# Reordering the opening of a one-core AdaLN transformer layer: split row load, another queue for one weight, stack transfers shared 6 and 6, value products placed among the row maxima, and a new written order for the first batch

## The reference

```python
mod = (silu(c) @ wmod)                      # 8 x 6 x 256: sa, ca, ga, sb, cb, gb
h = layernorm(x) * (1 + ca) + sa
qkv = h @ w_qkv                             # 16 heads of width 16
scores = q @ k.T / 16, causal, softmax      # 16 heads x 1024 x 1024
x = x + ga * ((softmax @ v) @ w_o)
h = layernorm(x) * (1 + cb) + sb
shared = (silu(h @ w1.T) * (h @ w2.T)) @ w3.T          # hidden 1024
routed = top 2 of 8 experts of hidden 256, gated by a sigmoid
x = x + gb * (shared + routed)
```

## Time and profile before

| What | us |
|---|---|
| median of 3 runs | 1855.86 |
| profiled execution, its own time | 1855.64 |
| its span, first to last instruction | 1853.8 |
| TensorE busy / VectorE busy / ScalarE busy / GpSimd busy | 1718.1 / 1580.6 / 1074.0 / 913.8 |
| mean granted TensorE clock | 0.964 |

### The profile page before, as it was taken

How to read it: one execution, slowest core, us unless ns; L and a number is a source line. 1 busy time by engine, 2 the same in 40 slices (tenths; PEclk the granted TensorE clock), 3 DMA queues, 4 the chain that set the end, 5 groups by cost and what they waited for, 6 DMA issues and landing times.

```text
span 1853.8 us, 46094 instructions
## 1 busy us (share of the span) xinstructions
PE 1718.1 (93%) x17630; PEld 992.5 (54%) x17630; DVE 1580.6 (85%) x2889; ACT 1074.0 (58%) x1346; POOL 913.8 (49%) x1003
## 2 busy tenths in 40 slices
PE   5578889999999999999999999999999999899896
PEld 2223445545554455545454545455544888678674
DVE  7889999998998898999889988998896777556787
ACT  2568767666766676767666766776665333222321
POOL 2123356455545654545545555546455467444433
PEclk8598899999999999999999999999999999999998
DMA  4234321303121312122212121222213667767998
GB/s 148 54 131 133 109 58 49 90 17 89 42 64 42 90 44 67 40 88 42 65 30 87 42 65 39 79 42 82 53 43 119 165 135 158 155 161 157 267 321 289
DMA packets 214133, 183.14 MB, mean 99 GB/s; under 512 B 146640, under 2 KB 182232, under 8 KB 212128
## 3 DMA queue, kind: packets, MB, share of 16 engines
q1 hardware_dynamic: 200768, 143.87, 30.4%
q0 software_dynamic: 12960, 36.06, 5.8%
q10 hardware_dynamic: 192, 0.26, 0.1%
HBM read 65.23 MB, written 62.19 MB: 69 GB/s over the span
## 4 chain that ended last, share of the span: by engine, by line
PE 54%; DVE 19%; POOL 8%; issue 6%; SPq 5%; DMA 5%; ACT 4%; ACTq 0%; DVEq 0%; POOLq 0%
PE pair L1892 11%; PE pair L1884 11%; DVE max_part L1319 9%; PE pair L1936 6%; PE pair L1862 6%; PE pair L1916 5%; PE pair L1838 5%; PE pair L1812 3%; POOL lists L983 3%; PE pair L1927 2%; PE pair L1824 2%; ACT arena L1129 2%; POOL slots L998 2%; PE pair L1962 1%; POOL hidden L1004 1%
## 5 line engine op out<-in xcount | busy, mean ns | idle before, releaser
L1129 ACT ACTIVATE arena<-pair 128x1024 f32<-128x1024 f32 (+1 forms) x640 | 570.1, 938 | 206.7 <-PE pair L1862 200.8
L1319 DVE TENSOR_REDUCE max_part<-pair 128x2 f32<-128x1024 f32 (+2 forms) x448 | 532.8, 1214 | 38.8 <-PE pair L1838 36.7
L1892 PE MATMUL pair<-feat_parts,ffn_sb 128*128 128x512 f16 x1536 | 379.1, 381 | 8.4 <-DVE silu_h L1367 2.9
L1884 PE MATMUL pair<-arena,v_sb 128*32 128x256 f32 (+1 forms) x5120 | 324.0, 374 | 3.4 <-POOL arena L916 1.5
L916 POOL TENSOR_SCALAR_AFFINE_SELECT arena<-arena 128x512 f32<-128x512 f32 x256 | 161.7, 647 | 228.9 <-ACT arena L1129 228.4
L922 POOL TENSOR_SCALAR_AFFINE_SELECT arena<-arena 128x1024 f32<-128x1024 f32 x128 | 141.3, 1104 | 248.8 <-ACT arena L1111 248.6
L1838 PE MATMUL pair<-arena 48*128 48x128 f16 (+3 forms) x2304 | 207.5, 284 | 34.8 <-DVE max_part L1319 10.6
L1862 PE MATMUL pair<-arena 50*128 50x256 f16 (+1 forms) x2560 | 212.8, 266 | 27.0 <-ACT arena L1129 13.9
L1892 PEld LDWEIGHTS pair<-feat_parts,ffn_sb 128*128 128x128 f16 x1536 | 130.8, 98 | 175.8 <-issue 29.9
L1916 PE MATMUL pair<-parts,arena 128*128 128x256 f16 x1704 | 201.3, 277 | 14.0 <-DMA parts<-lists 11.1
L998 POOL DMA_INDIRECT slots<-arena,feat x142 | 144.4, 1017 | 137.8 <-DVE arena L1556 105.6
(11 more groups left out here) (218 smaller groups left out, 2160.9 us busy)
## 6 DMA issues: line engine op xcount, KB each, us to landing
arena<-parts SPq DMA_DIRECT2D x380, 64.0 KB, 2.3
rows<-x SPq DMA_DIRECT2D x8, 1024.0 KB, 5.6
x_sb<-x SPq DMA_DIRECT2D x16, 512.0 KB
base<-norm SPq DMA_DIRECT2D x14, 512.0 KB, 3.3
ffn_parts<-hidden SPq DMA_DIRECT2D x8, 768.0 KB, 4.1
arena<-ffn_parts SPq DMA_DIRECT2D x8, 768.0 KB, 6.6
x_sb<-ffn_w SPq DMA_DIRECT2D x6, 768.0 KB, 5.5
norm<-ffn_w SPq DMA_DIRECT2D x6, 768.0 KB, 7.0
```

The lines of the kernel that those rows point to most:

```text
L1129: sc.activation(to[:, :, lo:QC], of[:, :, lo:QC], ACT.Exp, scale=SCALE / QK_SCALE ** 2).then_inc(exp_done, 1)
L1319: return vec.tensor_reduce(to, of, AX.X, ALU.max)
L1884: last = mm(to[32 * j:32 * j + 32, lo:QC], v_sb[:, kt, h:h + 32], probs[:, u % RING, at + lo:at + QC], start=(kt == 0), stop=(kt == 2 * c ...
L1892: last = mm(to[:, 0:512], w_up[s][W_PART[i]][:, f, m * RH + h * P:m * RH + (h + 1) * P], feat_parts[:, A_PART[i], f, c * 512:(c + 1) * 512 ...
```

## The change

- The rows of batch 0 come in two transfers of 512 KB, each with a semaphore, and the statistics of each half wait only for their own.
- `wmod_sb` is sent from ScalarE's queue, ahead of its first instruction, instead of from SyncE's.
- Of the 8 row tiles VectorE normalises 0 to 3, and ScalarE 4 to 7.
- The first 12 stack transfers go 6 and 6 (`FIRST_BY`).
- In the start, `v:0` and `v:1` stand behind the eighth maximum (`V_BEHIND = 8`) instead of ahead of the first; `take_v` stands behind `shifts`; `split` of group 1 stands between the maxima 3 and 4. The banks of the start are others.
- The order and the banks of "first" are others. "second" and all that follows is unchanged.

```diff
-FIRST_SENT = 4
+FIRST_BY = ((0, 6), (6, 12))
 "first":
-        max:1:0 max:1:1 max:1:2 max:1:3 share:0 share:1 select_max:1:1 qk:2 scores:0 max:1:4 max:1:5 scores:1 diag_max:1:1 scores:2 scores:3 values:0 values:1
-        raw:0 max:1:6 max:1:7 max:1:8 select_max:1:5 scores:4 diag_max:1:5 scores:5 scores:6 select_max:1:10 select_max:1:14 max:1:9 max:1:10 max:1:11
-        max:1:12 max:1:13 diag_max:1:10 max:1:14 scores:7 values:2 max:1:15 max:1:16 max:1:17 share:2 share:3 diag_max:1:14 values:3 values:4 values:5
-        values:6 scores:8 normalise:0 scores:9 raw:1 load_x1 shifts:1 max:2:0 scores:10 scores:11 scores:12 scores:13 values:7 values:8 values:9 values:10
-        values:11 raw:2 normalise:1 normalise:2 max:2:1 max_turn:1 mods scores:14 max:2:2 scores:15 values:12 scores:16 gates_out scores:17 values:13 guards
+        load_x1 select_max:1:1 max:1:0 max:1:1 max:1:2 max:1:3 max:1:4 share:0 qk:2 scores:0 scores:1 max:1:5 diag_max:1:1 raw:0 normalise:0 values:0 values:1
+        share:1 select_max:1:5 select_max:1:10 scores:2 scores:3 max:1:6 max:1:7 max:1:8 diag_max:1:5 max:1:9 scores:4 scores:5 max:1:10 max:1:11 scores:6
+        max:1:12 values:2 select_max:1:14 max:1:13 diag_max:1:10 max:1:14 values:3 values:4 max:1:15 max:1:16 max:1:17 share:2 share:3 scores:7 values:5
+        values:6 scores:8 scores:9 scores:10 scores:11 scores:12 values:7 values:8 diag_max:1:14 shifts:1 max:2:0 max:2:1 raw:1 normalise:1 values:9 values:10
+        values:11 scores:13 max_turn:1 mods scores:14 scores:15 scores:16 scores:17 scores:18 values:12 values:13 raw:2 normalise:2 values:14 values:15
+        values:16 guards scores:19 scores:20 scores:21 max:2:2 raw:3 select_max:2:1 values:17 values:18 values:19 max:2:3 raw:4 scores:22 values:20 values:21
...
-    "start": "0246024602460246024602460"
+    "start": "0246024024024026262626262"
...
-WORK["start"] = [("turn", 0), ("turn", 1), ("qk", 0), ("qk", 1), ("v", 0), ("v", 1)]
-WORK["start"] += [("max", 0, p) for p in range(MAXES)] + [("max_turn", 0)]
+V_BEHIND = 8
+WORK["start"] = [("turn", 0), ("turn", 1), ("qk", 0), ("qk", 1)] + [("max", 0, p) for p in range(V_BEHIND)]
+WORK["start"] += [("v", 0), ("v", 1)] + [("max", 0, p) for p in range(V_BEHIND, MAXES)] + [("max_turn", 0)]
...
 # SyncE
-            load_x1(0)
-            sp.dma_start(wmod_sb, w_mod[:, :, 0:2 * D]).then_inc(mod_in, 16)
+            for h in range(2):
+                t = slice(4 * h, 4 * h + 4)
+                sp.dma_start(rows[:, t, :], x_v[0][:, t, :]).then_inc(x1_first[h], 16)
...
-            stack(0, 0, FIRST_SENT)
+            sp.wait_ge(part_low, at_group(0, 0))
+            for to, of in first_stack(0):
+                sp.dma_start(to, of).then_inc(stacked[0], 16)
             stack(0, 1)
 # ScalarE
+            sc.dma_start(wmod_sb, w_mod[:, :, 0:2 * D]).then_inc(mod_in, 16)
...
+            act.wait_ge(std1_ready, 1)
+            for t in range(NT // 2, NT):
+                sc.activation(rows[:, t, :], rows[:, t, :], ACT.Identity, bias=rstd[:, 2, t:t + 1], scale=rstd[:, 1, t:t + 1]).then_inc(norm1_act, 1)
...
 # VectorE
-            dve.wait_ge(x1_in, 16)
             for h in range(2):
+                dve.wait_ge(x1_first[h], 16)
                 spread(0, rows, 4 * h, 4 * h + 4, var1_ready)
...
-            for g in range(EARLY):
-                split(0, "start", g)
-            for h in range(2):
-                take_v(0, "start", h)
+            split(0, "start", 0)
             for p in range(MAXES):
+                if p == 4:
+                    split(0, "start", 1)
                 if not OF_DIAG[p]:
                     maxima(0, "start", 0, p)
...
             shifts(0, 0, 0)
+            for h in range(2):
+                take_v(0, "start", h)
```

More of the change, by code:

```diff
@@ L138 @@
[L138 to L149, removed]
@@ new lines @@
+        scores:23 spread1:0 max:2:4 scores:24 scores:25 select_max:2:5 scores:26 diag_max:2:1 max:2:5 max:2:6 max:2:7 values:22 gates_out max:2:8 diag_max:2:5
+        select_max:2:10 values:23 share:4 scores:27 scores:28 spread1:1 scores:29 scores:30 values:24 values:25 values:26 values:27 max:2:9 max:2:10 max:2:11
+        max:2:12 max:2:13 diag_max:2:10 select_max:2:14 share:5 values:28 qk:3 normalise:3 normalise:4 values:29 max:2:14 values:30 scores:31 scores:32
+        scores:33 values:31 raw:5 raw:6 max:2:15 max:2:16 scores:34 scores:35 max:2:17 norm1 scores:36 values:32 load_gates diag_max:2:14 normalise:5
@@ new lines @@
+        normalise:6 scores:37 values:33 scores:38 turn:0 scores:39 values:34 values:35 values:36 shifts:2 select_max:3:1 max:3:0 max_turn:2 max:3:1 max:3:2
+        max:3:3 max:3:4 select_max:3:5 max:3:5 raw:7 diag_max:3:1 values:37 values:38 values:39 share:6 scores:40 scores:41 scores:42 turn:1 max:3:6 raw:8
+        values:40 values:41 max:3:7 scores:43 scores:44 max:3:8 diag_max:3:5 select_max:3:10 max:3:9 scores:45 max:3:10 max:3:11 share:7 select_max:3:14 qk:0
+        normalise:7 raw:9 values:42 scores:46 scores:47 values:43 values:44 values:45 scores:48 scores:49 max:3:12 max:3:13 diag_max:3:10 max:3:14 max:3:15
@@ new lines @@
+        scores:50 values:46 values:47 values:48 values:49 share:8 scores:51 scores:52 scores:53 max:3:16 values:50 normalise:8 normalise:9 scores:54 scores:55
+        scores:56 select_max:0:1 max:3:17 diag_max:3:14 raw:10 values:51 values:52 scores:57 values:53 shifts:3 max:0:0 max:0:1 scores:58 max_turn:3
+        normalise:10 values:54 values:55 max:0:2 max:0:3 share:9 qk:1 scores:59 scores:60 values:56 values:57 values:58 max:0:4 scores:61 scores:62 values:59
+        scores:63 scores:64 raw:11 diag_max:0:1 max:0:5 max:0:6 max:0:7 max:0:8 values:60 values:61 select_max:0:5 select_max:0:10 raw:12 share:10
@@ new lines @@
+        diag_max:0:5 max:0:9 max:0:10 v:0 v:1 scores:65 max:0:11 scores:66 normalise:11 max:0:12 share:11 load_x:0 values:62 values:63 scores:67 values:64
+        scores:68 scores:69 values:65 max:0:13 max:0:14 values:66 values:67 scores:70 scores:71 select_max:0:14 diag_max:0:10 max:0:15 values:68 max:0:16
+        scores:72 max:0:17 values:69 scores:73 raw:13 scores:74 values:70 scores:75 normalise:12 raw:14 normalise:13 values:71 normalise:14 diag_max:0:14
+        shifts:0 values:72 values:73 scores:76 scores:77 scores:78 values:74 scores:79 values:75 max_turn:0
@@ L356 @@
     assert next(banks, None) is None, v
-DVE_SETUP = 23
+DVE_SETUP = 22
 DVE_FIRST = 43
@@ L536, in adaln_layer @@
         x1_in, x_in = sem("x1_in"), [sem(f"x_in{h}") for h in range(2)]
+        x1_first, std1_ready, norm1_act = [sem(f"x1_first{h}") for h in range(2)], sem("std1_ready"), sem("norm1_act")
         gates_in, part_done, x_scaled = sem("gates_in"), sem("part_done"), sem("x_scaled")
@@ L1232, in _ @@
             act.wait_ge(part_low, at_group(0, 0))
[L1233 to L1236, removed]
+            for to, of in first_stack(1):
+                sc.dma_start(to, of).then_inc(stacked[0], 16)
             part_hi(0, "start", 1)
@@ L1648, in batch @@
                         if at[0] == 0:
[L1649 removed]
+                            dve.wait_ge(x1_in, (b + 1) * 16)
                             dve.wait_ge(feat1_ready, at_half(b, 1))
@@ L1680, in _ @@
             vec.tensor_copy(mod_sb, misc[0:B, :]).then_inc(setup_read, 1)
-            norm1(0, 0)
+            dve.wait_ge(inv1_ready, 1)
+            vec.scalar_tensor_tensor(rstd[:, 2, :], mean_var[:, :, 0], -1.0, rstd[:, 1, :], ALU.mult, ALU.mult).then_inc(std1_ready, 1)
+            dve.wait_ge(std1_ready, 1)
+            for t in range(NT // 2):
+                vec.tensor_scalar(rows[:, t, :], rows[:, t, :], rstd[:, 1, t:t + 1], rstd[:, 2, t:t + 1],
+                                  ALU.mult, ALU.add).then_inc(norm1_ready, 1 if t < NT // 2 - 1 else 1 + NT // 2)
             dve.wait_ge(setup_full, 2)
```

28 lines of the change are left out of this document (17 added, 11 removed).

## The result

The changed kernel took 1861.08 us (median of 15 runs, 1856.62 to 1868.63), the kernel before 1855.86 in 15 runs beside it (1849.75 to 1865.49). The ratio is 1.0036, 95% interval 1.0022 to 1.0050: 4 to 9 us slower, 6.7 by the ratio, against +1 forecast. It lies inside the range and inside the 0.5% that was called no change. Of the four values on record (1857, A 1868, B 1847, C 1860) C's is the nearest; by the ratio, 6.7 lies about midway between the forecast's +1 and A's +12. The profiled execution (span 1863.8 us, its own time 1865.58) lies 4.5 above the median, and that of before at its own; where they are compared with each other, differences of a few us late in the program are not to be read.

What follows compares the result with a forecast made beforehand. VectorE's idle time, 13.3 us in the opening and 15.4 in the first batch, was taken as the bound. Terms -2.0, -1.2, +6.0, +1.15 gave +4.0 at shifts, +5.0 after take_v and bank 2, order -4.0: +1.0, 1857; range 1846 to 1868.

Steps and rivals of the forecast that it cites:

- A: Rival, the stall stays: values at half clock throughout, first batch 7.5 us late, nothing given back; 1868; chance 0.2.
- B: Rival: start as forecast, but the new order removes nearly all VectorE's first-batch waits (12 us); 1847; chance 0.23.
- C: Rival: loads share one bandwidth, queue issuing collides, opening gains 0 instead of 3.2 us, same stall; 1860; chance 0.12.
- the forecast's own case: Whole kernel: the terms as forecast, 1857, with 1852 to 1862 for this case alone; chance 0.45.
- signs of being wrong: Values in 5.4 us at clock 1.00, or max_turn:0 of batch 1 over 6 us away from 214.
- signs of being right: Among them: statistics about 6.0, first maximum near 35.8, one idle of 5 to 7 us, shifts near 64, gates near 104.
- Front: Opening, up to ScalarE's scaling: halved rows, w_mod's other queue and four ScalarE tiles gain 2.0 us (0 to 2.4).
- Transfers six and six: Opening's stack transfers: two fewer issues on SyncE bring the first product 1.2 us earlier (0 to 1.3).
- The stall: Opening, behind the eighth maximum: VectorE idles 6.0 us while TensorE makes the values in 8.3 us.
- Into the first batch: Between shifts and the first batch's first maximum: take_v +2.4, wait for bank 2 +0.5, less the old 1.8 gap.
- The order: First batch up to the gates: the new order gives back 4.0 of the 5.0 us of lateness.
- if TensorE keeps up: First batch before the gates: TensorE's work, about 22 us at full clock, up to 30 at half, against VectorE's 25.3.

Runs made afterwards that it cites:

- e5: e1 with half the rows first on each queue, w_mod behind ScalarE's half, and the first batch's old order and banks: 1854.48 us, ratio 1.0006.
- e3: Kernel before with only the values behind the eighth maximum, the start's new banks, take_v behind shifts, split of group 1 between maxima: 1858.57 us, ratio 1.0024.
- e1: Changed kernel with values back ahead of the maxima, take_v before the first maximum, split of group 1 ahead: 1853.62 us, ratio 0.9993.
- e6: The same as e5, but with the new order of the first batch: 1853.81 us, ratio 1.0007.
- e8: Changed kernel with values and both splits ahead of the maxima, other start banks, take_v left behind shifts: 1856.92 us, ratio 1.0012.
- e9: e1 with the first batch's order and banks of the kernel before: 1852.81 us, ratio 0.9994.
- e10: e1 with each queue sending half of the rows, then half of w_mod, ahead of all else: 1853.36 us, ratio 0.9993.
- e4: Kernel before with only the new order and banks of the first batch, start untouched: 1853.53 us, ratio 0.9996.
- e2: Changed kernel with the first batch's order and banks of before, start as changed: 1858.18 us, ratio 1.0026.

## Why the prediction was right and where it was not

The range, the sign and the mechanism of the stall held; the size was 6.7 instead of 1. The range held because it was wide: the forecast's own case was put at 1852 to 1862, and 6.7 us by the ratio is 1862.5. One of its signs of being wrong came true: `max_turn:0` of batch 1 stands at 222.84 (212.91 before), more than 6 us from 214, in an execution 4.5 us above the median. Of the signs of being right, the gates near 104 (108.65) and VectorE's idle time (8.5 us more in the opening, not 5; 1.1 us more in the first batch, not 5 less) did not come. By its own steps:

- **Front, -2.0: it was -0.4** (`split` of group 0 at 28.74 against 29.14). The step that failed was "with half the bytes I let the first half start at 6.0". The first half began at 7.13, no earlier than the whole had, while w_mod's product began at 6.01 instead of 8.53. The rule quoted in the prediction from the Trainium skill, page "DMA: Bandwidth & Descriptors", section "Queues, rings and completion order", is that the DMA engines take turns between queues; the trace agrees in that w_mod gained and the rows did not, and e5 agrees from the other side. But I had drawn from it that nothing would be lost, since I took only the second half to be late; it was the first half too. Normalising began at 13.02, 1.1 us behind the 11.9 of the prediction, and the four tiles on ScalarE took 2.08 us, 0.52 each, where 0.4 was taken between 0.3 and 1.2, which is 0.5 us: together the 1.6 us that are missing. The 0.4 itself is near what the same opening varies by: in the three programs with the front of before, `split` of group 0 began at 29.14, 29.07 and 28.81, in the six with the new front and its loads at 28.35 to 28.74.

```profile
13.09 2.08 ACT L1246 ACTIVATE rows<-rows,rstd 128x256 f32<-128x256 f32 x4 [10.06 <-DVE rstd L1698]
15.89 1.20 ACT L1094 ACTIVATE o_tok<-pair,mod_col 128x1024 f32<-128x1024 f32 x1 [0.72 <-PE pair L1825]
```

- **Transfers six and six, -1.2: right as a number, but most of it is not the sharing.** From the first issue to the first product it is 36.91 - 29.99 = 6.92 us against 38.52 - 30.39 = 8.13. But e3 sends eight and four, with the values moved, and takes 37.59 - 30.33 = 7.26; and the six kernels that send six and six with the values ahead (e1, e5, e6, e8, e9, e10) take 7.30 to 7.80, mean 7.54. So the sharing is worth 0.3 to 0.7 us, and the rest of the 1.2, 0.9 us by e3, comes from the values' products no longer running beside the transfers. That was a term that the prediction put at nothing; the two errors cancel. With the products beside them one issue on each queue took 0.8 to 1.3 us longer than its neighbours (1.61 on SyncE, 1.92 on ScalarE in the kernel before, the others 0.59 to 0.77); why, no run shows. SyncE's queue in e1, then in the changed kernel, and the first product in e3 and e1:

```profile
29.67 5.75 SPq L889 DMA_DIRECT2D arena<-parts  x6
...
29.99 4.16 SPq L889 DMA_DIRECT2D arena<-parts  x6
```

```profile
37.59 1.46 PE L1840 MATMUL pair<-arena 48*128 48x512 f16 x12 [7.91 <-DMA arena<-parts]
...
37.47 1.05 PE L1862 MATMUL pair<-arena 48*128 48x512 f16 x16 [3.19 <-DMA arena<-parts]
```

- **The stall, +6.0: 5.38**, the values 7.80 instead of 8.3 us. Its place, releaser and cause are as forecast. The clock's part of it is 2.4 us, and it changes with the moment at which the clock rises (1.2 us in e3).
- **Into the first batch, +1.1 (2.4 + 0.5 - 1.8): 1.15** (68.41 - 65.45 against 62.06 - 60.25). Right in size; e8 shows that with this order's bank 2 `take_v` itself costs 0.4.
- **The order, -4.0: about 0.** This is the term that was mis-sized, and the step behind it that failed is "if TensorE keeps up". The 4.24 us wait ahead of the gates is gone, and in its place stands one of 3.16 us for `mods` (L2018). Against the old order, with one maximum of 1.13 us taken off it, the gates come 0.3 us (e4 against before), 0.5 (changed kernel against e2), 0.7 (e1 against e9) and 1.7 us (e6 against e5) earlier, not 4. The account of VectorE's work was right: from `raw:0` (79.50, forecast 77.8) to the gates (108.65, forecast 103.1) it worked 25.2 us, as the prediction's 25.3 (its "12" maxima are 14 in the list; the sum has them). What it lacked were 4.0 us of waits, 3.16 of them for `mods`, whose products began at 105.02, 2.8 us after `shifts:1` had ended at 102.20, and took 3.60 us:

```profile
79.50 0.45 DVE L1365 STREAM_TRANSPOSE o_raw<-pair 128x256 f32<-128x256 f32 x1 [1.79 <-PE pair L1909]
```

```profile
104.56 0.62 PE L1874 MATMUL pair<-ident_b,max_bf 128*8 128x128 f16 x8
105.02 3.60 PE L2018 MATMUL pair<-feat,choice 128*8 128x512 f32 x8
```

  TensorE had worked without a gap since 99.08; it was behind. I had let it "keep up" on the strength of 22 us at full clock, although its clock was 0.50 for much of that stretch in the profile of before (73.6 to 90.5 us), as it was in the changed kernel from 80 to 92. That the clock is what put it behind is argued, not shown: it also stood before that for ScalarE and VectorE (1.24 us ahead of 99.08, 1.11 ahead of 94.68), and no run changes the clock alone. The waits moved, and their sum stayed. The list of waits of the kernel after (65.5 to 222.9) has nearly as much as the earlier trace rows:

```profile
DVE max_part L1335 <- PE pair L1863: 6.6, 7, 2.1
DVE hidden L1424 <- PE pair L2018: 3.2, 1, 3.2
DVE o_raw L1365 <- PE pair L1909: 2.5, 3, 1.8
```

With the terms as measured (-0.4, -1.2, +0.2 for the first product, +5.4, +1.2, +1.1, 0) the sum is +6.3, and the ratio says 6.7. The idle time of VectorE was the right account to draw up; that idle time in the next stage would absorb lateness was the error in using it. Of the rivals, A put the price too high (12) but had the right rule, that nothing is given back, though not its condition, values at half clock throughout (7.80 us, not 10.8); C's 0 for the front was nearer than my 2.0, though its 1860 rests on the order giving 4 us back, which it did not.

Open: in three of four pairs of profiled executions the new order's first batch ends later than the old one's (4.8, 4.1, 2.5 and -1.2 us), while the ratios differ by -0.0004, +0.0010, -0.0001 and +0.0001. Whether it loses something that is given back later, or whether these are single executions with the clock falling at other places, the runs do not tell.

## What to carry to other kernels

Work of a fast engine that lies in the shadow of a transfer is nearly free (here the transfers took 0.4 to 0.9 us longer beside it), and the same work among the steps of a slower engine costs its own time less what that engine has in hand: count the buffers between the two (here two maxima, which covered 2.42 us) before a block of 5 us is put there, and price the block at the clock that the stretch grants, not at the one it had in its old place. Idle time of an engine in a later stage is no credit for lateness from an earlier one, unless one can name the wait that the lateness shortens. A load that was brought forward on another queue landed early, and the load that had been first gained nothing from being cut in half (7.13 against 7.06 us); look which of the two ends the wait before giving either the lead.

## What the runs showed of the hardware that was not expected

- Which load leads which queue: with the rows (1 MB) first on one queue and w_mod (0.5 MB) on the other, statistics began at 7.13 and w_mod's product at 6.01; with half of the rows first on each queue, 5.84 and 9.43; with everything on one queue, 7.06 and 8.53.
- The same 48 products took 6.60 and 7.80 us in the same place of two programs, and 5.40 ahead of the maxima, by how much of them fell to the clock level of 0.50. The clock had stood at 0.50 since 31.8 us when the 7.80 began; the 5.40 passed at 1.00.
- ScalarE needed 0.52 us for each tile of 256 columns (2.08 for 4) and 1.20 for one of 1024: four small operations cost 1.7 times the one that covers the same columns. (The four read SBUF, the one reads the products' `pair`, so the two differ in more than the width.)
- Twelve stack transfers of 64 KB, from the first issue to the first product that needs them: 8.13 and 8.29 us (eight and four) and 7.30 to 7.80 (six and six) with 48 products of TensorE beside them, 7.26 and 6.88 to 6.92 without.
